# One stream of score units over all attention jobs, where each job used to drain before the next began

## The reference

```
x = x + attn(cond(x))          # two attentions, one behind the other
x = x + ffn(cond2(x))          # a recurrent mixer, then a mixture of 8 experts and a shared expert
cond : out = softmax(Q K^T / 4 + bias, or over 32 listed keys per query) V, then Wo
attn : causal softmax(q k^T / 4) v, then W_proj
cond2: causal scans over the tokens, sigmoid gates, gelu, Wout, layer norm
ffn  : router, top 2 of 8 experts (capacity 320), silu(x Wg) * (x Wu) @ Wd; shared expert of width 2048
```

## Time and profile before

| | |
|---|---|
| median of 3 runs | 1787.53 us (1787.46 to 1789.6) |
| the profiled execution | 1797.83 us, span 1796.0 us |
| mean granted TensorE clock | 0.94 |
| busy: PE, DVE, ACT, POOL | 1625.0, 919.1, 742.1, 645.0 us |
| preparation, up to the first scores | about 0 to 130 us |
| attention, jobs 0 to 15 | about 130 to 1128 us |
| tail | 1128 to 1796 us |

### The profile page before, as it was taken

How to read it: one execution, slowest core, us unless ns; L and a number is a source line. 1 busy time by engine, 2 the same in 40 slices (tenths; PEclk the granted TensorE clock), 3 DMA queues, 4 the chain that set the end, 5 groups by cost and what they waited for, 6 DMA issues and landing times.

```text
span 1796.0 us, 20631 instructions
## 1 busy us (share of the span) xinstructions
PE 1625.0 (90%) x7632; PEld 771.4 (43%) x7632; DVE 919.1 (51%) x2045; ACT 742.1 (41%) x1028; POOL 645.0 (36%) x353
## 2 busy tenths in 40 slices
PE   5789899778989988887899988999999999999998
PEld 3433223223322322433343323545655566666655
DVE  6679688898658866445665552225312111111131
ACT  4744555455555555365555557233221111111111
POOL 5437889876788989031000000220001100000051
PEclk9569999999999999998899988999999999999999
DMA  3450213313131220244231002300030004233052
GB/s 103 141 140 24 60 33 86 88 44 83 44 78 33 67 48 7 72 123 145 74 74 42 22 22 83 119 15 0 0 141 6 19 1 169 86 128 128 14 103 39
DMA packets 72737, 121.42 MB, mean 68 GB/s; under 512 B 12009, under 2 KB 50354, under 8 KB 69308
## 3 DMA queue, kind: packets, MB, share of 16 engines
q1 hardware_dynamic: 68987, 113.61, 22.2%
q0 software_dynamic: 3072, 6.03, 1.9%
q10 hardware_dynamic: 576, 0.47, 0.1%
HBM read 85.08 MB, written 36.96 MB: 68 GB/s over the span
## 4 chain that ended last, share of the span: by engine, by line
PE 48%; DVE 5%; DMA 4%; ACT 4%; SPq 2%; POOL 2%; issue 2%; another core or an unknown queue 1%; ACTq 0%; DVEq 0%; POOLq 0%
PE wide L1962 19%; PE wide L1974 5%; PE wide L1980 5%; PE wide L1903 4%; PE wide L1880 3%; PE bank L1753 3%; DMA sb_den<-o_raw 2%; POOL sb_prob L1085 2%; PE bank L1852 2%; DVE sb_rowmax L1558 1%; ACT sb_prob L1287 1%; PE wide L1852 1%; DMA sb_xg<-slots_in 1%; PE bank L1745 1%; PE wide L1885 1%
## 5 line engine op out<-in xcount | busy, mean ns | idle before, releaser
L1085 POOL TENSOR_TENSOR sb_prob<-sb_prob,sb_weight 128x1024 f32<-128x1024 f32 x192 | 453.4, 2385 | 111.2 <-ACT sb_prob L1287 110.4
L1287 ACT ACTIVATE sb_prob<-wide 128x1024 f32<-128x1024 f32 (+3 forms) x384 | 348.5, 917 | 279.2 <-PE wide L1885 154.5
L1880 PE MATMUL wide<-sb_stack_q,sb_stack_k 99*128 99x512 bf16 (+3 forms) x896 | 299.0, 373 | 27.2 <-DVE sb_prob L1617 19.1
L1852 PE MATMUL bank<-sb_stack_k,sb_stack_q 96*128 96x512 bf16 (+3 forms) x596 | 220.3, 388 | 53.1 <-DVE sb_rowmax L1558 28.7
L1564 DVE CUSTOM_DVE_ANT_0 sb_junk<-bank,sb_bias 128x512 bf16<-128x512 f32 x339 | 225.8, 686 | 72.0 <-PE bank L1852 69.3
L1331 ACT ACTIVATE sb_sil<-wide 128x320 f32<-128x320 f32 (+1 forms) x128 | 66.2, 517 | 459.6 <-PE wide L1962 419.6
L1903 PE MATMUL wide<-sb_prob,sb_v_aug 128*17 128x512 f32 (+3 forms) x1792 | 231.1, 580 | 17.6 <-POOL sb_prob L1085 9.6
L1962 PE MATMUL wide<-sb_weight,sb_ffn 128*128 128x512 f32 x512 | 233.0, 598 | 0.0
L1709 DVE TENSOR_TENSOR sb_act_s<-sb_sil,wide 128x512 f32<-128x512 f32 x64 | 43.9, 686 | 268.3 <-ACT sb_sil L1331 242.4
L1558 DVE TENSOR_REDUCE sb_rowmax<-bank 128x1 f32<-128x512 f32 (+3 forms) x257 | 136.3, 553 | 74.0 <-PE bank L1855 41.6
L1962 PE MATMUL wide<-sb_xgT,sb_big 128*128 128x320 f32 x512 | 152.8, 444 | 1.1 <-ACT sb_xgT L1346 1.1
(11 more groups left out here) (258 smaller groups left out, 1946.4 us busy)
## 6 DMA issues: line engine op xcount, KB each, us to landing
sb_stack_k<-parts SPq DMA_DIRECT2D x32, 256.0 KB, 6.9
o_raw<-sb_o_raw SPq DMA_DIRECT2D x32, 256.0 KB, 2.2
sb_big<-rg SPq DMA_DIRECT2D x8, 1024.0 KB, 5.0
sb_big<-ru SPq DMA_DIRECT2D x8, 1024.0 KB, 7.1
sb_big<-rd SPq DMA_DIRECT2D x8, 1024.0 KB, 9.8
sb_stack_q<-parts SPq DMA_DIRECT2D x16, 384.0 KB, 5.0
parts<-sb_o_norm SPq DMA_DIRECT2D x48, 128.0 KB
sb_stack_q<-parts SPq DMA_DIRECT2D x16, 256.0 KB, 5.4
```

What stands on the lines that cost most here:

```text
L1085: e.tensor_tensor(p, p, weight_of(*u[1:]), ALU.mult).then_inc(weigh_p.handle, 1)
L1287: e.activation(p[:, :, first:HALF], sc[:, :, first:HALF], ACT.Exp).then_inc(SC.empty_sem(u), 1)
L1852: i = e.matmul(bk[:, 0:hi - lo], stack_q[0:ROWS, n % 3, h, qt * P:(qt + 1) * P], stack_k[0:ROWS, n % 3, h, lo:hi], start=True, stop=not diag)
L1880: i = e.matmul(sc[:, j * HALF + first:(j + 1) * HALF], stack_k[0:ROWS_M, n % 3, g, kt * P:(kt + 1) * P], stack_q[0:ROWS_M, n % 3, g, half ...
```

## The change

The plan is written over one queue of all units of all jobs. Each round i issues the scores of unit i and the value product of unit i - 4, whichever jobs they belong to. So there is a drain only behind the last job. `o` of a job's second half now stands in the next job's round 4. `behind_job` collects the loads and steps that follow a job: its loads are put out in round 5 (`PV_LAG + 1`) of the next job, and its extra steps are spread from `opened = ends[4]` to 0.9 instead of from 0 to 0.9 (`opened` is 5/32 = 0.156 in a prior job and 0.219 in a causal one). The values `v` of a new batch start in round 4 instead of 0. The maxima, finishing steps and `turn` keep their places. In the loads before job 9 and job 10 `stack` now comes first. `ffnload` moves from round 4 of job 15 to behind its last score. No instruction is added or removed.

```diff
--- before.py
+++ after.py
@@ -338,71 +338,91 @@
     return [("y" if att == 0 else "resid", b, mc, half) for mc in range(DC) for half in range(NH)]
 
 
+def behind_job(n):
+
+    att, b, q = JOBS[n]
+    loads, units = [], []
+    if n == 1:
+        loads.append(("late_loads",))
+    if (att, b, q) == (1, 0, 0):
+        loads.append(("mixload",))
+    if (att, b, q) == (1, 0, 1):
+        loads += [("woload",), ("zero",)]
+    stage = STAGES[q]() if att and b and q in STAGES else []
+    if q % 2 and n + 1 < len(JOBS):
+        gap, later = (stage[:len(stage) // 2], stage[len(stage) // 2:]) if stage else (GAP, GAP)
+        units += [("num", att, b, q // 2)] + gap + [("inv", att, b, q // 2)] + later + [("times", att, b, q // 2)]
+    else:
+        units += stage
+    if q == NQ - 1 and n + 1 < len(JOBS):
+        units += GAP + outputs(att, b)
+    return loads, units
+
+
 def attention_plan():
+
 
     plan = []
     extras, more = halves(projection(0, 1))
-    late = []
-    for n, (att, b, q) in enumerate(JOBS):
+    late, behind, begun = [], [], -1
+    queue = [(n, u) for n in range(len(JOBS)) for u in range(units_of(n))]
+    for i in range(len(queue) + PV_LAG):
+        n, u = queue[i] if i < len(queue) else (len(JOBS) - 1, units_of(len(JOBS) - 1) + i - len(queue))
+        att, b, q = JOBS[n]
         causal = att == 1
-        next_weights = (att, b, q) == (0, 0, NQ - 1)
-        if n + 2 < len(JOBS):
-            plan.append(("stack", n + 2))
-        values = [("v", att, b, kt) for kt in range(NT)] if q == 0 else []
-        if (att, b, q) == (0, 1, 0):
-            values.append(("w2load",))
         last = units_of(n)
-        cost = [250 + 2 * (HALF - first_of(n, *place(n, u)[:2])) for u in range(last)]
-        ends = [sum(cost[:u + 1]) / sum(cost) for u in range(last)]
-        steps = [(0.9 * k / len(extras), 0, k, f) for k, f in enumerate(extras)]
-        steps += [(at, 1, k, f) for k, (at, f) in enumerate(max_stream(n))]
-        steps = [(at, f) for at, _, _, f in sorted(steps)]
-        extras, more = more, []
-        for u in range(last + PV_LAG):
-            if n + 1 == len(JOBS) and u == PV_LAG:
-                plan += [("ffnload", k) for k in range(EARLY)]
+        if n != begun:
+            begun = n
+            values = [("v", att, b, kt) for kt in range(NT)] if q == 0 else []
+            if (att, b, q) == (0, 1, 0):
+                values.append(("w2load",))
+            cost = [250 + 2 * (HALF - first_of(n, *place(n, k)[:2])) for k in range(last)]
+            ends = [sum(cost[:k + 1]) / sum(cost) for k in range(last)]
+            opened = ends[PV_LAG] if n else 0
+            loads = [("stack", n + 2)] if n + 2 < len(JOBS) else []
+            if n:
+                front, units = behind_job(n - 1)
+                loads += front
+                extras += units
+                if JOBS[n - 1][0] == 0 and JOBS[n - 1][2] == NQ - 1:
+                    one, more = halves(projection(1, JOBS[n - 1][1]))
+                    extras += one
+            steps = [(opened + (0.9 - opened) * k / len(extras), 0, k, f) for k, f in enumerate(extras)]
+            steps += [(at, 1, k, f) for k, (at, f) in enumerate(max_stream(n))]
+            steps = [(at, f) for at, _, _, f in sorted(steps)]
+            extras, more = more, []
+        if i == len(queue):
+            plan += [("ffnload", k) for k in range(EARLY)]
+        if u == (PV_LAG + 1 if n else 0):
+            plan += loads
+        if u >= PV_LAG or not n:
             plan += values[:2 if causal else 1]
             values = values[2 if causal else 1:]
-            now = []
-            while steps and (u >= last or steps[0][0] < ends[u]):
-                now += flat([steps.pop(0)[1]])
-            plan += now[:1]
-            if u < last:
-                plan.append(("score", n, u))
-            if 0 < u <= last and not causal and not to_pool(n, u - 1):
-                plan.append(("weigh", n, u - 1))
-            plan += now[1:]
-            if u >= PV_LAG and u - PV_LAG < last:
-                half, kt, pair = place(n, u - PV_LAG)
-                if pair == PAIRS_OF - 1:
-                    plan.append(("pv", n, half, kt))
-                    if next_weights:
-                        late += [(n, u, ("kw_load", 1, kt, half)), (n, u + 2, ("kw", 1, kt, half)),
-                                 (n, u + 3, ("kw_sum", 1, kt, half))]
-                        late.sort()
-                elif kt == 0 and half:
-                    plan.append(("o", n, 0))
-            while late and (n - late[0][0]) * units_of(late[0][0]) + u >= late[0][1]:
-                plan.append(late.pop(0)[2])
-        plan.append(("o", n, 1))
-        stage = STAGES[q]() if att and b and q in STAGES else []
-        if q % 2 and n + 1 < len(JOBS):
-            gap, later = (stage[:len(stage) // 2], stage[len(stage) // 2:]) if stage else (GAP, GAP)
-            extras += [("num", att, b, q // 2)] + gap + [("inv", att, b, q // 2)] + later + [("times", att, b, q // 2)]
-        else:
-            extras += stage
-        if n == 1:
-            plan.append(("late_loads",))
-        if (att, b, q) == (1, 0, 0):
-            plan.append(("mixload",))
-        if (att, b, q) == (1, 0, 1):
-            plan += [("woload",), ("zero",)]
-        if q == NQ - 1 and n + 1 < len(JOBS):
-            extras += GAP + outputs(att, b)
-            if att == 0:
-                one, more = halves(projection(1, b))
-                extras += one
-    return first_plan() + with_splits(flat(plan + extras), SPLIT_AT)
+        now = []
+        while steps and (u >= last - 1 or steps[0][0] < ends[u]):
+            now += flat([steps.pop(0)[1]])
+        plan += now[:1]
+        if i < len(queue):
+            plan.append(("score", n, u))
+        if 0 < i <= len(queue):
+            m, v = queue[i - 1]
+            if JOBS[m][0] == 0 and not to_pool(m, v):
+                plan.append(("weigh", m, v))
+        plan += now[1:]
+        if i >= PV_LAG:
+            m, v = queue[i - PV_LAG]
+            half, kt, pair = place(m, v)
+            if pair == PAIRS_OF - 1:
+                plan.append(("pv", m, half, kt))
+                if JOBS[m] == (0, 0, NQ - 1):
+                    late += [(i, ("kw_load", 1, kt, half)), (i + 2, ("kw", 1, kt, half)), (i + 3, ("kw_sum", 1, kt, half))]
+                    late.sort()
+            elif kt == 0 and (m or half):
+                plan.append(("o", m, 0) if half else ("o", m - 1, 1))
+        while late and i >= late[0][0]:
+            plan.append(late.pop(0)[1])
+    plan.append(("o", len(JOBS) - 1, 1))
+    return first_plan() + with_splits(flat(plan), SPLIT_AT)
 
 
 def route_plan(b):
```

## The result

The changed kernel takes **1806.2 us** (median of 5 runs, 1802.94 to 1807.68); the kernel before, over 5 runs, 1789.6 us (1787.46 to 1794.24). The ratio is **1.0075, 95% interval 1.0053 to 1.0098**: slower, by 9.5 to 17.5 us. Forecast was 1780, with 1762 to 1797 as the range. Both the sign and the range were wrong. The profiled execution took 1805.14 us (span 1803.0), that of before 1797.83.

What follows compares the result with a forecast made beforehand. POOL was taken to set the pace in prior jobs, PE or chains over DRAM in causal ones. From the median of 1787.53, -27 + 3 + 3.5 + 3 + 2 + 4 + 3 + 1 = -7.5 gave 1780 us, range 1762 to 1797.

Steps and rivals of the forecast that it cites:

- A: Boundaries into jobs 1 to 7: POOL's pauses before its first weighings vanish; -27 us, from 13.3 to 29.8 gained.
- E: Job 12: longer stall for denominators, +2 us, from 0 to 3.7; job 4's growing stall covered by POOL's units, no cost.
- Rival 1: Prior jobs: the gaps only move in jobs 1, 4 and 5, A gives 13.3; +6, 1794 us, chance 0.15.
- B: Job 8: division of job 7 hangs on an `o` behind five units; +3 us, from -3.5 to +7.
- H: After PE's waits: longer waits meet PE's lowered clock more often; +1 us, up to +3.
- C: Job 9: ScalarE's third product step waits longer for the first one's parts; +3.5 us, from 0 to 5.7.
- D: Job 10: `num` and `inv` lie closer, so DVE waits longer for denominators; +3 us, from 0 to +5.
- F: Jobs 13 to 15: the mixer's steps start five units later; +4 us for the three, from 0 to 9.
- G: Causal half: a second half's `o` stands between exponentials and PE's value product waits; +3 us, from 0 to 4.
- I: Loads: `stack` five units later and `ffnload` behind the store at 1105.37 are covered; cost 0.
- Rival 3: Causal jobs, set by chains from the store, lose their five units whole: 41 against 27, +14, 1801.5 us, chance 0.13.
- Rival 2: Causal chains have slack: C to F are nothing, G stays; -27 + 3, 1763.5 us, chance 0.20.

Runs made afterwards that it cites:

- e3: Kernel before with the stream at the boundaries into jobs 1 to 7 alone, weight blocks loaded early: 1779.44 us, ratio 0.9934.
- e9: As e3, but `stack(5)` is loaded in round 12 of job 3 instead of round 5: 1774.45 us, ratio 0.9906 to the kernel before.
- e1: Changed kernel with the first two shared-expert weight blocks loaded in round 4 of job 15 again: 1802.89 us, ratio 1.0059 to the kernel before.
- e6: As e3, with the stream also into jobs 8, 10, 12 and 14: 1788.66 us, ratio 0.9982 to the kernel before.
- the standard: Profile of e2, used as a second profile of the kernel before's attention order: span 1786.4 us, ratio 1.0001.
- e4: Kernel before with the stream at the boundaries into jobs 8 to 15 alone, weight blocks loaded early: 1811.25 us, ratio 1.0099.
- e2: Kernel before with only the first two weight blocks loaded late, behind the last score of job 15: 1791.72 us, ratio 1.0001.
- e12: Kernel before with the stream into job 15 alone, weight blocks loaded early: 1794.68 us, ratio 1.0025.
- e14: As e9, but the loads of jobs 8, 10, 12 and 14 go out in round 8 instead of 0: 1782.91 us, ratio 0.9949.
- the best kernel found here: As e9, extra steps of jobs 1, 5, 7 spread from 0; in job 10 `stack` in round 1, `woload` and `zero` in round 16: 1771.22 us, ratio 0.987.

## Why the prediction was wrong

- **A, the prior boundaries: -27 forecast, -12 measured (e3, 8 to 16).** This is the step that failed. The pauses at the boundaries did vanish almost wholly, as said, and A's own lower end was 13.3. What failed is the choice of nine tenths of the upper end, "because POOL runs without a break soon after the start": it looked at POOL's pauses alone, 29.8 us of them, and POOL's idle time fell by 14. Five units moved ahead of the last `o` also move the rounds that follow it, and every load whose *use* is tied to a round comes that much sooner, while its *issue* is tied to the `o` and to the queue. The text costed `stack` as a load that is itself needed late; it never asked what stands behind `stack`. That is `priorT` in job 3: moving `stack(5)` out of its way gave 5 us (e9 against e3, with intervals that overlap), together with a higher clock of PE in job 3. With that one load moved, the prior boundaries are worth 17 us (e9, 0.9906). The other 10 us to the forecast stay open. Two places are seen: the table in job 2 (4.66 us of wait; but e1, e6 and e9 have the same wait and a job 2 of 64.5 us, 3 us shorter than the standard's 67.5, so the wait alone doesn't set it), and job 4, where E said that three POOL units would cover the longer stall and POOL's wait grew by 2.6 us.
- **Rival 1 came nearest in the size of A**: A at 13.3 and the other terms as they are, +6, 1794, chance 0.15. It had the size and not the jobs. It expected the gain to be lost in jobs 1, 4 and 5. Against the standard, jobs 1, 5 and 6 are shorter by 6.3, 4.6 and 6.6 us, and jobs 2 and 3 longer by 1.7 and 8.5.
- **B to H, the causal boundaries: +19.5 forecast, +18 measured (e4), +22 between e3 and e1.** Right as a sum. By parts: job 8 is longer by more than B says (7.7 against 3, its upper end was 7). C is right on the products (13.4 us from the first to the third, 13.6 forecast) but the wait grew only from 3.77 to 5.09, not to 7; job 9 lost nothing. D and E forecast waits "near 15" and 2 us more: 15.09 and 5.83, and the jobs are 2.7 and 4.4 us longer against 3 and 2. The product rows would have given 13.5 and not 13.6 (17.28 x 3072/4608 is 11.5), which changes nothing. F forecast 4. From `o` to `o` jobs 13 to 15 are 3.2 us shorter together, but job 15 is then counted without its first five units; from first exponential to first exponential they are 3.5 us longer, near F. G forecast 3: in the profile PE waits 0.45 us for the `o` of a second half at four of the boundaries, 1.8 us in all.
- **H, the clock: +1 forecast, too small.** Over the causal half PE's time lost (as in the table above) is 23 to 32 us (mean 29) in the eight profiles that stream into jobs 8, 10 and 12, and 20 to 28 (mean 24) in the twelve others. That is 5 us, near the 6.5 that the prediction worked out for three growing waits beside the Trainium skill (TensorE: Matmul & The Clock Gate, "HAM oscillation") and set aside because the waits of jobs 8 and 10 "pay already". By jobs, the means differ by +3.1 us in job 8, -0.4 in job 9 and +1.4 in job 12, then +2.0 in job 13, -2.4 in job 14 and +0.9 in job 15. So of the three waits job 8's is paid for, job 12's in part and job 9's not. In job 10, where DVE's wait grew by 3.2 us and PE's from 11.89 to 13.14, the low clock behind it is as long as before: in the changed kernel PE starts again at 854.14 and has its full clock from 859.1 on, before it started at 858.73 and had it from 863.8 on, 5 us each. The windows, the changed kernel's and then the one of before that follows:

```profile
853.00:856.00 3.00, 1.85 (x7) 0.95 (x8) 2.51 (x8) 0.47 (x1) 0.00 (x0) 0.50 0.05 11
856.00:860.00 4.00, 4.00 (x19) 1.18 (x18) 2.32 (x6) 1.81 (x3) 0.00 (x0) 0.61 0.55 151
```

```profile
862.00:866.00 4.00, 4.00 (x24) 1.37 (x22) 2.23 (x7) 2.10 (x3) 0.00 (x0) 0.78 0.58 166
```

- **I, the loads: 0 forecast.** Right for `ffnload` in the order of before (e2, ratio 1.0001), not settled in the stream (e1), and wrong for `stack`, as told under A.
- **The tail, "isn't touched by the change".** In the profile it is 9 to 10 us longer (677 against 668 and 667). e2 has the late load and a tail of 667.2 us, e12 streams into job 15 and has 667.1, and e9 does neither and has 674.2: neither the load nor the last boundary alone brings this about; see below. Whether the changed kernel meets the long form more often (its five runs have a mean clock of 0.932 to 0.934, those of the kernel before beside the experiments 0.939 to 0.952) no run shows.
- **Rival 3** had 1801.5 and the right sign, by losses of 41 us against 27. The losses were 18 to 22, against 12: near its time for another reason. **Rival 2** (C to F at nothing) was refuted by the waits themselves; its sum also left out B and H, with which it would be -20, 1767.5.
- **A page against a row.** The fit of the Trainium skill (DMA: Bandwidth & Descriptors, "Anatomy of one DMA") is given for DMAs issued by GpSimd; here SP issues them. Taken for this load, as in the prediction's estimate of 3.3 us, it would have the denominators arrive in time. The trace differs once more: 15.09 us of waiting in job 10. In e14, where the same load is issued ahead of `stack`, DVE doesn't wait for it.

With A at -12 and the causal boundaries, the clock among them, at +18 to +22, the sum is +6 to +10; 9.5 to 17.5 was measured. The rest is not explained by a run; the two overlap within their intervals, and the longer tail in the profile shows that PE's clock may hold a part of it.

## What to carry to other kernels

When units are moved across a boundary, list each load whose consumer is counted in rounds and whose issue hangs on something else, with everything that stands ahead of it on its queue. A pause taken from one engine is a gain only as far as nothing else is due in the same time: cost it from the lower end unless each job has been looked at. Count the same units in both kernels before two stretches are compared: a mark like `o` that itself moved makes job 15 look shorter when it is longer. And drains are not all alike: in the best kernel found here the drain stands where a long chain over DRAM starts at its end, and the chain's own loads go first in the queue (job 10 is 7.5 us shorter for that in the profile).

## What the runs showed of the hardware

- **One tail, three lengths.** With PE busy without a break, its granted clock fell to half a few microseconds into the tail in some profiles and not in others, for identical plans of job 15 and the tail (e3 and e9 above). PE's time lost over the tail and the tail's length go together: 2.4 to 3.3 us and 666.0 to 667.9 in twelve profiles, 6.1 and 669.9 to 671.0 in four, 9.7 and 673.4 to 677.2 in four, the changed kernel's among them. Thus a single profile can be 7 us off for a reason that no row of the change explains. Whether the changed order makes the long form more likely is open, with one profile of each kernel. In the changed kernel:

```profile
1120.00:1126.00 6.00, 6.00 (x45) 2.12 (x43) 0.00 (x0) 1.63 (x5) 0.00 (x0) 0.55 0.00 0
1126.00:1132.00 6.00, 6.00 (x34) 4.14 (x33) 0.68 (x2) 2.28 (x3) 0.00 (x0) 1.00 0.76 238
1132.00:1140.00 8.00, 8.00 (x19) 4.21 (x19) 0.74 (x4) 0.23 (x1) 0.00 (x0) 0.57 0.81 276
1140.00:1146.00 6.00, 6.00 (x21) 3.80 (x20) 4.38 (x38) 3.78 (x5) 0.00 (x0) 1.00 0.17 59
```

- **Where a load stands in the queue can decide when it lands.** In e9 DVE waits 5.0, 12.1 and 1.9 us for denominators in jobs 8, 10 and 12. In e14, where only the round of the loads ahead of them is another, none of these waits is left. The first `priorT` load of job 3 lands 6.9 us after its issue behind the seven loads of `stack(5)`; later ones of the same size in the same job land after 1.7 to 2.2 us.
- **The spread of the runs goes with the clock.** The eight runs of e1 reach from 1783.9 us at a mean clock of 0.944 to 1807.8 at 0.932: 24 us for one kernel. The profile of e1 (span 1781.7) is its fastest run and would have misled alone.
